# Mixture-of-experts stage of a two-layer decoder: the gates reach the 128 partitions by DMA from DRAM rows instead of by a TensorE product and a ScalarE copy

## The reference, cut to what matters

```python
def _L1_ffn_ref(x, router_w, up_w, down_w):
    router_logits = jnp.einsum('bsd,de->bse', x, router_w)
    routing_weights = jax.nn.softmax(router_logits, axis=-1)
    topk_weights, topk_indices = jax.lax.top_k(routing_weights, K)      # K = 4 of 8
    topk_weights = topk_weights / jnp.sum(topk_weights, axis=-1, keepdims=True)
    h = jnp.einsum('bsd,edh->bseh', x, up_w)                            # 128 -> 512
    h = jax.nn.gelu(h)
    expert_outputs = jnp.einsum('bseh,ehd->bsed', h, down_w)            # 512 -> 128
    gathered = jnp.take_along_axis(expert_outputs, topk_indices[:, :, :, None], axis=2)
    return jnp.sum(topk_weights[:, :, :, None] * gathered, axis=2)
...
x = x + _L1_ffn_ref(_layernorm(x, axis=-1), L1_ffn_router_w, L1_ffn_up_w, L1_ffn_down_w)
```

## Time and profile before

| | us |
|---|---|
| median of 3 runs | 2997.16 |
| lowest and highest of the runs | 2996.25, 3002.15 |
| the profiled execution, its own time | 3003.07 |
| its span, first to last instruction | 3001.2 |
| TensorE matmuls, busy | 2651.9 (88% of the span) |
| VectorE, busy | 2357.9 (79%) |
| ScalarE, busy | 1901.2 (63%) |
| GpSimd, busy | 1133.4 (38%) |
| DMA, mean over the span | 9 GB/s |

### The profile page before, as it was taken

The page is one execution under the profiler, slowest core; times in us unless marked ns, Lnnn a source line. Parts: engine busy times, 40 slices in busy tenths (PEclk is TensorE's granted clock), DMA queues, the critical chain, the costliest instruction groups (busy, mean ns, idle before and its releaser), DMA issues.

```text
span 3001.2 us, 97587 instructions
## 1 busy us (share of the span) xinstructions
PE 2651.9 (88%) x36618; PEld 1996.7 (67%) x36618; DVE 2357.9 (79%) x6371; ACT 1901.2 (63%) x3499; POOL 1133.4 (38%) x965
## 2 busy tenths in 40 slices
PE   2999953867888888888899998999989999999998
PEld 2666632546777777777566665666767777777776
DVE  7999999777899999998699998666676666666665
ACT  1777752545566666665466665666667777777776
POOL 0333344008899999998233222444230000000000
PEclk9999975977999999999899999999789999999999
DMA  5000000000000000000100000000000000000000
GB/s 160 1 0 0 0 15 0 1 0 3 1 0 0 0 0 0 0 0 0 58 0 0 0 0 3 16 16 16 7 1 1 1 14 0 0 14 0 14 0 14
DMA packets 28702, 26.67 MB, mean 9 GB/s; under 512 B 4304, under 2 KB 23504, under 8 KB 28496
## 3 DMA queue, kind: packets, MB, share of 16 engines
q1 hardware_dynamic: 28624, 25.63, 2.9%
HBM read 21.43 MB, written 4.19 MB: 9 GB/s over the span
## 4 chain that ended last, share of the span: by engine, by line
PE 82%; DVE 9%; issue 5%; DVEq 1%; ACT 1%; POOL 1%; DMA 0%; ACTq 0%; POOLq 0%; SPq 0%
PE ps L1070 8%; PE ps L896 8%; PE ps L1059 5%; PE ps L1186 5%; PE ps L919 4%; PE ps L934 4%; PE ps L907 4%; PE ps L1084 4%; PE ps L1188 4%; PE ps L1155 4%; PE ps L1187 4%; PE ps L1157 4%; PE ps L1156 4%; DVE work L1612 3%; PE ps L947 2%
## 5 line engine op out<-in xcount | busy, mean ns | idle before, releaser
L470 POOL TENSOR_TENSOR work<-work,consts_sb 128x1024 f32<-128x1024 f32 x192 | 365.0, 1901 | 751.2 <-ACT work L602 590.1
L1070 PEld LDWEIGHTS ps<-work 32*32 32x32 f32 x16384 | 244.0, 145 | 122.9 <-issue 121.2
L1070 PE MATMUL ps<-work 32*32 32x32 f32 x16384 | 249.8, 226 | 72.6 <-DVE work L1612 59.5
L1755 DVE TENSOR_TENSOR h_low<-consts_sb,h_up 128x1024 fp32r<-128x1024 f32 x128 | 158.2, 1236 | 188.2 <-ACT h_up L797 188.2
L722 ACT ACTIVATE ps<-work 128x128 f32<-128x128 f32 x512 | 154.6, 354 | 232.0 <-DVE work L1594 220.9
L896 PE MATMUL ps<-work 128*128 128x512 f32 x512 | 262.4, 614 | 3.1 <-issue 0.2
L1186 PE MATMUL ps<-h_low,d_up 128*128 128x512 f32 x512 | 214.4, 419 | 0.6 <-DVE h_low L1755 0.5
L1155 PE MATMUL ps<-a_low,w_up 128*128 128x512 f32 x512 | 203.4, 397 | 0.9 <-DVE a_low L1730 0.9
L1188 PE MATMUL ps<-h_up,d_low 128*128 128x512 f32 x512 | 200.4, 391 | 0.0
L1157 PE MATMUL ps<-a_up,w_low 128*128 128x512 f32 x512 | 200.4, 391 | 0.0
L1156 PE MATMUL ps<-a_up,w_up 128*128 128x512 f32 x512 | 200.3, 391 | 0.0
(11 more groups left out here) (270 smaller groups left out, 6889.8 us busy)
## 6 DMA issues: line engine op xcount, KB each, us to landing
ctxT_all<-in_ctxT SPq DMA_DIRECT2D x1, 4096.0 KB, 12.9
work<-in_ctx SPq DMA_DIRECT2D x64, 64.0 KB, 1.8
out<-x_all SPq DMA_DIRECT2D x4, 1024.0 KB, 5.1
big<-in_up SPq DMA_DIRECT2D x1, 2048.0 KB, 8.4
consts_sb<-in_consts SPq DMA_DIRECT2D x1, 936.0 KB
w<-in_key_inT SPq DMA_DIRECT2D x1, 512.0 KB, 3.9
w<-in_key_out SPq DMA_DIRECT2D x4, 128.0 KB, 4.0
rows_sb<-in_rows SPq DMA_DIRECT2D x1, 384.0 KB
```

What stands on the lines that cost most here:

```text
L470: pool.tensor_tensor(KX[:, u].rearrange("p g (h k) -> p g h k", h=PER_SET), KC[:, u].unsqueeze(2).to_broadcast([P, SETS, PER_SET, SEQ]), o ...
L1070: ins = pe.matmul(psW[rows, n // 16, :, n % 16], XT[rows, T.u, :, n], YT[rows, T.u, :, n], start=True, stop=True)
L1755: dve.tensor_tensor(h_low[:, n], hid[n], h_up[:, n].bitcast(F32), ALU.subtract).then_inc(h_split, 1)
```

## The change

The gates are no longer split in upper and lower parts: `lw` itself is collected, turned to 8 rows of 512 tokens, and copied to `gT` in f32. SP stores these rows in a DRAM tensor (`gate_rows`, 16 KB per group). Then, for each expert, SP loads one row with a stride of zero over the partitions, so that it lands on all 128 of them (256 KB), in one of four slots of `GB`. `spread_gates` on TensorE, `keep_gates` on ScalarE and the preparation on VectorE are gone. `weighted` waits for the DMA of its slot. `gates` no longer waits for the down projections of the group two back but for the store of its rows. x is stored in 16 parts of 256 KB instead of four of 1 MB, in SP's list of segments.

```diff
-        gates_at = work[:, lg_at:lg_at + NT * 2 * MOE].rearrange("p (t n) -> p t n", n=2 * MOE)
...
-        gT = sb("gates_turned", [P, 2, WIDE], F32R)
-        prod, acc, GB = sb("weighted", [P, WIDE]), sb("summed", [P, 2, WIDE]), sb("gates_spread", [P, 2, WIDE])
-        pick = sb("pick_expert", [P, MOE], F32R)
+        gT = sb("gates_turned", [P, 2, WIDE])
+        prod, acc, GB = sb("weighted", [P, WIDE]), sb("summed", [P, 2, WIDE]), sb("gates_spread", [P, SLOTS, WIDE])
+        gate_rows = nc.dram_tensor("gate_rows", [NT // QUAD, MOE, WIDE], F32).ap()
...
-            parts = 4
-            for n in range(parts):
-                a, b = n * NT // parts, (n + 1) * NT // parts
-                sp.wait_ge(out_ready, b // QUAD)
-                sp.dma_start(ov[:, a:b, :], xs[:, a:b, :]).then_inc(stored, 16)
-            sp.wait_ge(stored, 16 * parts)
+
+            def keep_gate_rows(T):
+                sp.wait_ge(gT_ready, T.now())
+                sp.dma_start(gate_rows[T.t], gT[0:MOE, T.u, :]).then_inc(rows_out, 16)
+
+            def spread_gates(T):
+
+                sp.wait_ge(rows_out, T.step(16, 16))
+                for e in range(MOE):
+                    need(sp, prod_ready, T.step(MOE, e + 1 - SLOTS))
+                    sp.dma_start(GB[:, e % SLOTS, :], gate_rows[T.t, e].unsqueeze(0).to_broadcast([P, WIDE])).then_inc(gb_in[e % SLOTS], 16)
+
+            def store(T):
+                sp.wait_ge(out_ready, T.now())
+                sp.dma_start(ov.rearrange("p (s t) d -> p s t d", t=QUAD)[:, T.t], xs_quad[:, T.t]).then_inc(stored, 16)
+            staggered(nc, sp, NT // QUAD, [(0, keep_gate_rows), (0, spread_gates), (2, store)])
+            sp.wait_ge(stored, 16 * (NT // QUAD))
...
-            def keep_gates(T, e):
-
-                act.wait_ge(gb_done, T.step(MOE, e + 1))
-                need(act, prod_ready, T.step(MOE, e - 1))
-                act.activation(GB[:, e % 2], psGB, ACT.Copy).then_inc(gb_ready, 1)
...
-            def spread_gates(T, e):
-                if e == 0:
-                    pe.wait_ge(gT_ready, T.now())
-                need(pe, gb_ready, T.step(MOE, e))
-
-                pe.matmul(psGB, pick[0:2 * MOE, e:e + 1].to_broadcast([2 * MOE, P]), gT[0:2 * MOE, T.u, :], start=True, stop=True)\
-                    .then_inc(gb_done, 1)
...
                 if first:
-                    spread_gates(T, e)
                     need(pe, prod_ready, T.step(MOE, e - 1))
...
-            pe.wait_ge(pick_ready, 1)
...
-            dve.tensor_copy(lw_up[:, :, :], lw)
-            dve.tensor_copy(pick[:, :], C("pick"))
-            dve.drain()
-            dve.tensor_copy(gates_at[:, :, 0:MOE], lw_up[:, :, :].bitcast(F32))
-            dve.tensor_tensor(gates_at[:, :, MOE:2 * MOE], lw, lw_up[:, :, :].bitcast(F32), ALU.subtract).then_inc(pick_ready, 1)
-            dve.drain()
             dve.sem_inc(phase, 1)
...
-                need(dve, down_done, T.step(STEPS, -STEPS))
-                dve.tensor_copy(gT[0:2 * MOE, T.u, :], psGT).then_inc(gT_ready, 1)
+                need(dve, rows_out, T.step(16, -16))
+                dve.tensor_copy(gT[0:MOE, T.u, :], psGT).then_inc(gT_ready, 1)
...
-                dve.wait_ge(gb_ready, T.step(MOE, e + 1))
-                dve.tensor_tensor(prod[:, :], psD[e % 2], GB[:, e % 2], ALU.mult).then_inc(prod_ready, 1)
+                dve.wait_ge(gb_in[e % SLOTS], T.step(16 * MOE // SLOTS, 16 * (e // SLOTS + 1)))
+                dve.tensor_tensor(prod[:, :], psD[e % 2], GB[:, e % SLOTS], ALU.mult).then_inc(prod_ready, 1)
```

More of the change, by code:

```diff
@@ L159, in build @@
         ident = C("ident")
-        WORK = 18944
+        WORK = 19200
         work_space = ExitStack()
@@ L264, in build @@
         RING = 2
+        SLOTS = 4
         STEPS = 2 * MOE
@@ L286, in build @@
         w_up, d_up = sb("w_up", [P, MOE, HID], F32R), sb("d_up", [P, MOE, HC, P], F32R)
-        lw_up = sb("lw_up", [P, NT, MOE], F32R)
-        gT = sb("gates_turned", [P, 2, WIDE], F32R)
-        prod, acc, GB = sb("weighted", [P, WIDE]), sb("summed", [P, 2, WIDE]), sb("gates_spread", [P, 2, WIDE])
-        pick = sb("pick_expert", [P, MOE], F32R)
-        assert lg_end + 4 * WIDE + 2 * MOE * HID + NT * MOE + 7 * WIDE + MOE <= WORK
+        gT = sb("gates_turned", [P, 2, WIDE])
+        prod, acc, GB = sb("weighted", [P, WIDE]), sb("summed", [P, 2, WIDE]), sb("gates_spread", [P, SLOTS, WIDE])
+        assert lg_end + 4 * WIDE + 2 * MOE * HID + (5 + SLOTS) * WIDE <= WORK
+        gate_rows = nc.dram_tensor("gate_rows", [NT // QUAD, MOE, WIDE], F32).ap()
         ps = es.enter_context(nc.psum_tensor("ps", [P, 8, 512], F32))
@@ L325, in build @@
         psU = [ps[:, 2 * n:2 * n + 2, :] for n in range(RING)]
-        psD, psGB = [bank(4 + n, 0, WIDE) for n in range(2)], bank(6, 0, WIDE)
-        gates_of = t64[:, 0:8, :].rearrange("p n t -> p (n t)")[:, 0:2 * QUAD * 2 * MOE].rearrange("p (u t n) -> p u t n", u=2, t=QUAD)
-        psGT = ps[0:2 * MOE, 7, 0:WIDE]
+        psD = [bank(4 + n, 0, WIDE) for n in range(2)]
+        gates_of = t64[:, 0:8, :].rearrange("p n t -> p (n t)")[:, 0:2 * QUAD * MOE].rearrange("p (u t n) -> p u t n", u=2, t=QUAD)
+        psGT = ps[0:MOE, 7, 0:WIDE]
         psB = bank(7, 0, WIDE).rearrange("p (t d) -> p t d", t=QUAD)
@@ L384, in build @@
         a_step, a_split, w_step, w_split = sem("a_step"), sem("a_split"), sem("w_step"), sem("w_split")
-        pick_ready, g_turned, gT_ready, g_ready = sem("pick_ready"), sem("gates_turned_done"), sem("gates_turned_ready"), sem("gates_taken")
+        g_turned, gT_ready, g_ready, rows_out = sem("gates_turned_done"), sem("gates_turned_ready"), sem("gates_taken"), sem("gate_rows_out")
         up_done, hid_ready, h_up_ready, h_split, down_done = (
             sem("up_done"), sem("hidden_ready"), sem("hidden_up_ready"), sem("hidden_split"), sem("down_done"))
-        gb_done, gb_ready = sem("gates_spread_done"), sem("gates_spread_ready")
+        gb_in = [sem(f"gates_spread{n}_in") for n in range(SLOTS)]
         prod_ready, acc_done, back_done, out_ready = sem("prod_ready"), sem("acc_done"), sem("back_done"), sem("out_ready")
@@ L810, in between @@
                     gelu(T, k)
-                    if k % 2 == 0:
-                        keep_gates(T, k // 2 - 1)
                     upper_half(T, k)
-            staggered(nc, act, NT // QUAD, [(0, of(gelu, 0)), (1, of(keep_gates, MOE - 1)), (0, of(upper_half, 0)), (0, between)])
+            staggered(nc, act, NT // QUAD, [(0, of(gelu, 0)), (0, of(upper_half, 0)), (0, between)])
         @block.tensor
@@ L1730, in halves @@
                 dve.tensor_tensor(a_low[:, u, :], cT_quad[:, T.t, :], a_up[:, u, :].bitcast(F32), ALU.subtract).then_inc(a_split, 1)
-            gates_quad = gates_at.rearrange("p (s t) n -> p s t n", t=QUAD)
+            gates_quad = lw.rearrange("p (s t) n -> p s t n", t=QUAD)
             def take_gates(T):
```

## The result

The changed kernel took 2911.98 us (median of 4 runs, 2907.47 to 2916.01) against 2998.22 us before (4 runs). The ratio is 0.9709 with a 95% interval of 0.9694 to 0.9723, so 86.2 us faster by the medians. The forecast was 2910.9 us.

What follows compares the result with a forecast made beforehand. TensorE's matmul starts, 0.227 us apart and broken once per expert by the gate-repeating product, were taken as the bound; 81.9 + 1.75 + 2.6 = 86.3 us off the median 2997.16 gave 2910.9 us, range 2904 to 2926.

Steps and rivals of the forecast that it cites:

- Part 1: Experts stage, TensorE: removing the product that repeats the gates gives back 0.64 us for each of 128 experts, 81.9 us.
- the second wait: Even step's down projection waits for two semaphores (prod_ready, h_split), the odd one for one; priced at nothing, at most 12.8 us.
- Part 2: Experts stage, ScalarE: removing its copy of 590 ns is worth nothing by itself, as it is off the path.
- Part 3: Experts stage: the DMAs for the gates cost 0, landing in 2.4 us (bounds 1.8 and 8.4) under 20.7 us of cover.
- The straight line: Landing estimates for 256 KB: 2.4 us for a spread, between 64 KB and 2048 KB; 2.5 for a store, between 64 and 1024 KB.
- The allowance of 1 us at the start: Start of the experts stage: 1 us of loss allowed if two long h_low of VectorE beside GpSimd's weight halves follow each other.
- Part 4: Before the experts phase, VectorE: removing the preparation's copies from the chain of waits gives back 1.75 us (bounds 0.9 and 2.2).
- Part 5: End of the kernel: the last store shrinks from 1024 KB to 256 KB, giving back 2.6 us (bounds 0 and 3.3).
- A: Rival: only the product's own slot comes back, waits cause the irregular starts in even steps; gain 29.1 plus 4.3, 2963.8 us; 5%.
- B: Rival: the ring of up, gelu, halves and down becomes the bound, TensorE waits for h_low; about 2952 us; 3%.
- C: Rival: slower, reads of one DRAM row are serialised and the weighted product waits for its spread; 3213 us at 30 us landing; 3%.
- D: Rival: no gain, the chip grants TensorE a lower clock once its stream has no breaks, mean 0.89 in the stage; 1%.

## Why the prediction was right

- **What bounds the kernel.** Right: the starts of the matmuls, not the busy share. In the stretch 81.5 us came from TensorE's rhythm.
- **Part 1, 0.64 us per product, 81.9 us.** Confirmed from both sides: 81.5 us left with the change, 81.3 came back with the product alone. That the second wait costs nothing held: even steps start 0.23 us after the up projection. The column rule of the Trainium skill's page "TensorE: Matmul & The Clock Gate", section "Back-to-back issue gap", which would have given 27.6 us, is right for the product of 128 rows (28.2 us measured) and 54 us short for the one of 16. That section of the Trainium skill calls the rule the gap of an isolated matmul and gives about 131 ns per matmul of 512 columns as sustained; no run here shows that, the stream stands at 227 ns. The Trainium skill's page "TensorEngine Tiling (Array Packing)", section "Key Properties", says that changing the tiling mode drains the engine. The two runs with 128 rows agree with it; they show the price of going to 16 rows and back, 81.3 - 28.2 = 53.1 us over 128 times, 0.41 us, but not what happens in the array, nor that 16 rows are another tiling mode. The reason that the prediction gave, the late load of the product's weights, is half of what the traces show: the load behind it, of 128 rows, is late too, and with 128 rows in the product both run ahead. What holds them back stays open.
- **Part 2, the copy at nothing.** Right (726.6 us with and without).
- **Part 3, the DMAs at nothing.** Right in the sum; the landing was mis-sized. The straight line gave 2.4 us for a spread and 3.1 was measured; other rows of another tensor landed in 2.6. For the store it gave 2.5, and the median was 3.5 beside the spreads, but 2.3 for the last, which is alone: 1.9 of SP's wait and 0.4 of issue. The allowance of 1 us at the start, while GpSimd makes the lower halves, was about right: TensorE waits 1.3 us for h_low there, where the kernel before shows 0.5 at most. Its wait (waits from 2190 to 2220 of the profile after: us, times, longest):

```profile
PE ps L1179 <- DVE h_low L1741: 1.3, 2, 0.8
```

  Another 1.0 us of this kind stands at the last expert, which the prediction had not.

- **Part 4, 1.75 us.** 1.7 measured.
- **Part 5, 2.6 us.** 2.8 in the change's own profile, 2.7 when undone. (SP's last wait was foretold as 2.3 us, though 4.7 less 2.6 is 2.1; it was 1.9.)
- **The sum.** 86.3 foreseen, 86.0 in the profiles, 86.2 between the medians. That the medians agree to 0.1 us is luck, as the four runs of the changed kernel span 8.5 us. The range was rounded outward: its own terms give 2906.7 to 2923.7. The profiled execution came out at 2907.47 us and not at 2916.8, since the stages ahead of the change were 9.6 us shorter in it than in the profile of before.
- **The rivals.** A fell by the product alone. B: ScalarE cost nothing even at 82% busy, and TensorE waited for h_low at the two ends of the stage only. C: the landing of 3.1 us is far under the 20.7 at which it would decide; only with one slot and 1 MB per spread did the DMAs stand at the limit. D: the granted clock stayed at 1.00 with the stream full.

## What to carry to other kernels

In a dense stream of matmuls read the distance between starts, one period with and without the suspected instruction: it gives the price of an instruction, which neither its record nor the busy share does. A matmul over 16 rows in a stream of 128-row ones was dear here; padded with zero rows up to 128 it cost no more than its columns, which got back two thirds of its price before any of the work was moved elsewhere. (Other heights than 16 and 128 were not tried.) A DMA that repeats rows over the partitions was a free replacement where it could be issued an operation or more ahead. The first and the last of them are the ones to check, as they have the least cover: the first waited when other DMAs stood before it, the last when there was one slot.

## What was not expected of the hardware

- A 16-row matmul of 512 columns costs 81.3/128 = 0.64 us among 128-row ones, one of 128 rows 28.2/128 = 0.22 us.
- 128 packets that read one 2 KB row of DRAM landed in 3.1 us, 128 that read different rows of another tensor in 2.6 us. Which of the two differences counts was not tested.
- A spread of 1 MB in 8 KB packets landed in 4.7 us, four times the bytes for 1.6 us more than 256 KB in 2 KB packets, every 5.44 us (1 MB per period, about 190 GB/s), and the stretch, with its 3072 matmuls, grew by 5 us only, 4.5 of them at the last expert.
